# Moving the scaling and the PSUM reads of a quantised feed-forward stage from VectorE to ScalarE

## The reference, cut to what matters

```python
def act_quant(x):
    scale = 127.0 / jnp.clip(jnp.max(jnp.abs(x), axis=-1, keepdims=True), 1e-05)
    return jnp.clip(jnp.round(x * scale), -128, 127) / scale
def bit_linear(x, w):            # wq: ternary weights times one scale
    return jnp.einsum('bsd,hd->bsh', act_quant(x), weight_quant(w))
h = bit_linear(x, w1)                      # 1024 -> 4096
h = silu(depthwise_conv1d(h, conv_w, conv_b))   # 3 taps along the sequence
return bit_linear(h, w2)                   # 4096 -> 1024
# and then: x = layernorm(x + that)
```

## Time and profile before

| | us |
|---|---|
| median of the runs shown (6380.81 and 6395.15) | 6387.98 |
| the profiled execution | 6394.97 |
| its span, core 5, first to last instruction | 6393.4 |
| spans of the eight cores | 6309.8 to 6393.4 |
| from the first memset of the tile loop (4062.6) to the end | 2331 |
| one tile, from one store of y to the next (289.5 each) | 8 of them |

### The profile page before, as it was taken

One profiled execution on the slowest core, in us unless ns is written; L12 is line 12 of the kernel. 1 busy time (PEld: TensorE's weight loads), 2 busy tenths in 40 slices (PEclk: granted clock), 3 DMA queues, 4 the chain that ended last, 5 costly groups with the idle time before them and its releaser, 6 DMA issues.

```text
span 6393.4 us, 40611 instructions; the slowest of 8 cores (6309.8 to 6393.4 us)
## 1 busy us (share of the span) xinstructions
PE 2245.9 (35%) x11808; PEld 1178.4 (18%) x11808; DVE 1953.2 (31%) x3386; ACT 875.4 (14%) x1647; POOL 1499.9 (23%) x1336
## 2 busy tenths in 40 slices
PE   1345432653644543555740000123323232313333
PEld 0111110221211211222320000113222121212222
DVE  0013342332333343221143332233333333333332
ACT  0000032332322223211030000000000000000010
POOL 0000030110110123333241212133333423333333
PEclk8665555776766775777865555556665665656665
DMA  9840034003011010000105332300000000000000
GB/s 154 100 56 0 1 58 113 1 22 84 1 50 49 1 54 14 14 14 14 27 14 209 143 118 89 126 0 14 0 14 7 7 14 0 14 0 14 1 7 7
DMA packets 129593, 258.94 MB, mean 41 GB/s; under 512 B 16705, under 2 KB 79298, under 8 KB 124482
## 3 DMA queue, kind: packets, MB, share of 16 engines
q1 hardware_dynamic: 78786, 202.23, 9.9%
q0 software_dynamic: 50592, 54.11, 6.5%
HBM read 268.22 MB, written 42.21 MB: 49 GB/s over the span
## 4 chain that ended last, share of the span: by engine, by line
PE 33%; DVE 19%; DMA 17%; POOL 16%; issue 8%; ACT 6%; DVEq 1%; SPq 1%; POOLq 0%; ACTq 0%; another core or an unknown queue 0%
PE p4pm L120 8%; PE psm L120 7%; PE p3psv L120 6%; POOL p4tB L136 5%; POOL p4tA L136 4%; DMA xkv<-xT 4%; DVE p4tA L136 3%; DMA wqsw2T<-w2T 3%; POOL XB L136 3%; DVE Y L136 2%; DVE X L136 2%; DMA wqsw1T<-w1T 2%; DMA qbuf<-qTw 2%; PE p4pt L123 1%; DMA p4x<-xspill 1%
## 5 line engine op out<-in xcount | busy, mean ns | idle before, releaser
L136 POOL TENSOR_TENSOR p4tB<-p4h,cw 128x512 f32<-128x512 bf16 x256 | 330.9, 1292 | 553.1 <-DVE p4h L136 310.9
L136 POOL TENSOR_TENSOR Y<-Y,p2asb 128x416 f32<-128x416 f32 x120 | 144.4, 1236 | 1225.0 <-ACT p2bsb L127 1225.0
L120 PE MATMUL p4pm<-p4xq,w1q 128*128 128x260 bf16 x2048 | 260.6, 293 | 430.7 <-DVE p4h L136 415.9
L120 PE MATMUL p4pm<-p4c,w2q 128*128 128x256 bf16 x2048 | 245.8, 287 | 312.0 <-DVE p4c L140 312.0
L120 PE MATMUL p3psv<-XB,w3w 128*128 128x416 bf16 x1280 | 276.8, 386 | 191.4 <-POOL XB L136 190.9
L120 PEld LDWEIGHTS p4pm<-p4xq,w1q 128*128 128x128 bf16 x2048 | 208.6, 104 | 482.8 <-issue 435.0
L120 PEld LDWEIGHTS p4pm<-p4c,w2q 128*128 128x128 bf16 x2048 | 209.8, 103 | 351.6 <-issue 317.6
L136 DVE TENSOR_TENSOR p4tA<-p4tA,p4tB 128x512 f32<-128x512 f32 x256 | 177.1, 692 | 292.4 <-POOL p4tB L136 292.2
L123 PE MATMUL p4pt<-idenb,p4c 128*128 128x128 bf16 x512 | 64.8, 306 | 505.8 <-ACT p4c L132 423.1
L136 POOL TENSOR_TENSOR XB<-X,a3sb 128x416 bf16<-128x416 f32 x160 | 164.8, 1063 | 309.0 <-ACT a3sb L127 309.0
L136 POOL TENSOR_TENSOR p4tA<-p4c,p4tB 128x512 f32<-128x512 bf16 x128 | 148.1, 1157 | 369.7 <-ACT p4tB L127 224.1
(11 more groups left out here) (255 smaller groups left out, 4320.4 us busy)
## 6 DMA issues: line engine op xcount, KB each, us to landing
xkv<-xT POOLq DMA_DIRECT2D x32, 1024.0 KB, 16.9
wqsw1T<-w1T SPq DMA_DIRECT2D x16, 2048.0 KB, 9.3
wqsw2T<-w2T SPq DMA_DIRECT2D x64, 512.0 KB, 3.6
qbuf<-qTw SPq DMA_DIRECT2D x96, 256.0 KB, 3.8
sbuf<-sTe SPq DMA_DIRECT2D x96, 256.0 KB, 4.4
xspill<-X SPq DMA_DIRECT2D x2, 8320.0 KB, 26.9
X<-xin SPq DMA_DIRECT2D x1, 8320.0 KB, 47.1
xrb<-xspill SPq DMA_DIRECT2D x5, 1664.0 KB, 10.6
```

The lines of the kernel that those rows point to most:

```text
L120: e.matmul(o, l, r, start=s, stop=p), inc, 1)
L136: e.tensor_tensor(o, a, b, p), inc, 1)
```

## The change

Everything is in `emit_phase4`.

1. The product with the dequantising scale leaves the read of PSUM and goes into the last step of each quantisation: the tensor-scalar that subtracted MAGIC becomes a scalar-tensor-tensor, `(x - MAGIC) * scale`, both for `xq` (8 per tile) and for `cbuf` (16 per tile).
2. The reads of PSUM become plain copies on ScalarE: 32 per tile for the first product, 8 for the second. For the first two of each half, ScalarE waits for the convolution (`p4cv`) where VectorE did.
3. The casts of x and those of y4n, 8 and 8 per tile, are all done by ScalarE. VectorE and GpSimd no longer wait for them; GpSimd gets a wait for `p4xd` in `p4_front_b`.
4. The no-op and the semaphore `p4yb` go. In the convolution the waits for `p4he` and (new) `p4oe` stand only at `qq` = 0; in the later steps only that for `p4cq` is left. In the quantisation of `cbuf` GpSimd waits for `p4cq` only at `qq` = 0.
5. One memset gets a semaphore, and VectorE waits for it once.

```diff
-        engs = ("scalar", "vector", "gpsimd")
-        for eng in engs:
-            k.wait(eng, "p4xd", vx)
-            k.wait(eng, "p4hm", k.val("p4hm"))
-            k.wait(eng, "ns_qs", k.val("ns_qs"))
+        k.wait("scalar", "p4xd", vx)
+        k.wait("scalar", "p4hm", k.val("p4hm"))
+        k.wait("scalar", "ns_qs", k.val("ns_qs"))
         for ch in range(DCH):
-            k.cp(engs[ch % 3], xq[b][:, ch * TW:(ch + 1) * TW],
+            k.cp("scalar", xq[b][:, ch * TW:(ch + 1) * TW],
                  xc[b][:, ch * TW:(ch + 1) * TW], inc="p4cst")
...
-            k.tsc("vector", xq[b][:, ch * TW:(ch + 1) * TW], sl, MAGIC, None,
-                  ALU.subtract, inc="p4qa0")
+            k.stt("vector", xq[b][:, ch * TW:(ch + 1) * TW], sl, -MAGIC,
+                  rb1[b][:, TW:2 * TW], ALU.add, ALU.mult, inc="p4qa0")
...
-                k.wait("vector", "p4hm", k.val("p4hm"))
+                k.wait("scalar", "p4hm", k.val("p4hm"))
                 if hc16 < 2:
-                    k.wait("vector", "p4cv", k.val("p4cv"))
-                k.tt("vector", hbuf[:, hc16 * TW:(hc16 + 1) * TW], pm[:],
-                     rb1[b][:, TW:2 * TW], ALU.mult, inc="p4he")
+                    k.wait("scalar", "p4cv", k.val("p4cv"))
+                k.cp("scalar", hbuf[:, hc16 * TW:(hc16 + 1) * TW], pm[:], inc="p4he")
...
                 for eng in ("vector", "gpsimd"):
-                    k.wait(eng, "p4he", vhe)
+                    if qq == 0:
+                        k.wait(eng, "p4he", vhe)
+                        k.wait(eng, "p4oe", k.val("p4oe"))
                     k.wait(eng, "p4cq", k.val("p4cq"))
-                    k.wait(eng, "p4yb", k.val("p4yb"))
...
-            k.wait("gpsimd", "p4cq", vcq)
+            if qq == 0:
+                k.wait("gpsimd", "p4cq", vcq)
...
-            k.tsc("vector", c3, tA3, MAGIC, None, ALU.subtract, inc="p4hqw")
+            k.stt("vector", c3, tA3, -MAGIC, r3b, ALU.add, ALU.mult, inc="p4hqw")
...
-            k.wait("vector", "p4om", k.val("p4om"))
-            k.wait("vector", "p4yb", k.val("p4yb"))
-            v1 = k.tt("vector", tB[:, 0:OW], pm[:, 0:OW], tB[:, 3 * OW:4 * OW], ALU.mult,
-                      inc="p4oe")
+            k.wait("scalar", "p4om", k.val("p4om"))
+            k.wait("scalar", "p4y", k.val("p4y"))
+            v1 = k.cp("scalar", tB[:, 0:OW], pm[:, 0:OW], inc="p4oe")
...
-            k.wait("vector", "p4y", k.val("p4y"))
-            k.nopi("vector", "p4yb")
...
-        engs = ("scalar", "vector", "gpsimd")
-        for eng in engs:
-            k.wait(eng, "p4y", vy)
+        k.wait("scalar", "p4y", vy)
         for ch in range(DCH):
-            k.cp(engs[ch % 3], xq[b][:, ch * OW:(ch + 1) * OW],
+            k.cp("scalar", xq[b][:, ch * OW:(ch + 1) * OW],
                  y4n[:, ch * OW:(ch + 1) * OW], inc="p4yc")
```

More of the change, by code:

```diff
@@ L1369, in emit_phase4 @@
     k.memset("vector", cmt[:], 0.0)
-    k.memset("vector", cmtF[:], 0.0)
+    k.memset("vector", cmtF[:], 0.0, inc="p4mz")
+    k.wait("vector", "p4mz", k.val("p4mz"))
     def p4_front_a(t):
@@ L1417, in p4_front_b @@
         vcm = k.val("p4cmd")
+        k.wait("gpsimd", "p4xd", k.val("p4xd"))
         k.wait("vector", "p4red", k.val("p4red"))
@@ L1589, in p4_back @@
             r4b = tB[:, 2 * OW:3 * OW].unsqueeze(1).broadcast_to([128, 2, OW])
+            r3b = tB[:, 3 * OW:4 * OW].unsqueeze(1).broadcast_to([128, 2, OW])
             c3 = cbuf[:].rearrange("p (c w) -> p c w", c=32)[:, q0:q0 + 2, :]
             tA3 = tA[:].rearrange("p (c w) -> p c w", c=2)
-            k.wait("gpsimd", "p4cq", vcq)
+            if qq == 0:
+                k.wait("gpsimd", "p4cq", vcq)
             k.wait("gpsimd", "p4hqw", k.val("p4hqw"))
```

## The result

| | before | after |
|---|---|---|
| median of all runs | 6372.44 us (10 runs, 6356.57 to 6395.15) | 6430.91 us (11 runs, 6416.61 to 6454.37) |
| the profiled execution's span | 6393.4 us | 6415.1 us (core 4) |
| one tile, store to store, mean of 8 cores | 289.23 us (288.8 to 289.7) | 296.14 us (295.7 to 296.5) |

The ratio is 1.0095 with a 95% interval of 1.0077 to 1.0112. On the median before this is +60 us, between +49 and +71. The forecast was +62 and a time of 6450, in a range of 6415 to 6488.

A forecast was written before the change was run, and what follows sets the result against it. The prediction took the kernel to be bound by a serial chain of engines taking turns, none full. Its terms summed to +61.8 us, 6456.8 on the profiled execution, forecast as 6450 us against the runs' median; range 6415 to 6488.

The forecast's parts named there:

- Quantisation of cbuf: Second VectorE link of each step, 427 ns, becomes a 692 ns scalar-tensor-tensor, 128 times, all on the path: +33.9 us.
- Of xq: The same swap at 260 columns, 296 to 428 ns, 64 times: +8.4 us; bounds 0 and +13.6.
- Casts of x and y: Eight casts in a row on ScalarE end later than on three engines: +11.4 us for x, +11.0 for y.
- The side effect on the norm's sums: Norm's matmuls start later after the y casts, so more run at TensorE's slow clock: +1 us.
- Restart: Second half's first product: ScalarE must finish the last Silu before the read that lets TensorE go on: +5.1 us.
- Waits: Convolution steps 1 to 7: one wait fewer behind the blocking one, 0.07 us each, 112 times: -7.8 us.
- Reads: PSUM reads moved to ScalarE are hidden behind TensorE; only the last of each half gain: -1.2 us.
- starving: First product's steady chunks: ScalarE's reads hold up TensorE, +22 us, or +190 with lower clock; chances 0.03 up to +128, 0.03 over.
- Cancelling: Scalar-tensor-tensor as fast as the tensor-scalar in both quantisations: 20 us left, about +4 with waits at bound; chance 0.11.
- A gain of over 2%: Would take -128 us; VectorE's 256 removed PSUM reads, 109 us, all on the path wouldn't suffice; chance 0.01.

The follow-up runs named there:

- The run without the second tensor: Changed kernel with the last step of both quantisations a tensor-scalar again, the dequantising scale left out; ratio 1.0005 (0.9983 to 1.0028).

## Why the stages can't hide each other: the chain cut

The quantisation of cbuf has one scratch tile `tA`, while the first half of `tB` lies idle. With both in turn GpSimd can multiply for the next step while VectorE rounds.

```diff
-            tA3 = tA[:].rearrange("p (c w) -> p c w", c=2)
-            k.wait("gpsimd", "p4hqw", k.val("p4hqw"))
+            tQ = tA[:] if qq % 2 == 0 else tB[:, 0:QW4]
+            tA3 = tQ.rearrange("p (c w) -> p c w", c=2)
+            k.wait("gpsimd", "p4hqw", k.val("p4hqw") - (2 if qq > 0 else 0))
```

Both roundings work on `tQ` too. In the kernel before, the edit also leaves GpSimd's wait for `p4cq` at step 0 alone, as the change does. In the changed kernel and in the kernel before:

> The changed kernel with two scratch tiles in turn in the quantisation of cbuf, so that GpSimd multiplies for the next step while VectorE rounds this one. If the two engines truly overlap, a step takes about 1.3 us (GpSimd 1.16, VectorE 0.43 + 0.69 and gaps) instead of 2.64, -170 us, and the scalar-tensor-tensor costs nearly nothing. If they hold each other up, as the 1.04 us GpSimd operation of the convolution that takes 1.56 beside VectorE suggests, a step takes the sum of the busy times, 2.28: -46 us.

> The kernel before with the same two scratch tiles. Overlapping: 1.25 us a step instead of 2.37, -140 us. Holding each other up: 1.16 + 0.43 + 0.43 = 2.02 a step, -45 us. Beside the run of the changed kernel with two tiles this gives the price of the scalar-tensor-tensor where the chain is cut: about 0.05 us a step if they overlap, 0.26 if they don't.

Measured: 0.9939 (0.9921 to 0.9957) for the changed kernel with two tiles, 0.9841 (0.9817 to 0.9865) for the kernel before with two tiles: 99 us and 101 us gained, by the ratios; by the tile it is 87 and 84 us over eight. The distance between the two versions is still 0.98%. A step takes neither of the values I gave. Timelines of the kernel before, then of the changed kernel, each with two tiles:

```profile
4547.23 1.21 POOL L136 TENSOR_TENSOR p4tB<-p4c,p4tB 128x512 f32<-128x512 bf16 x1 [0.43 <-DVE p4c L140]
4547.53 1.19 DVE L140 TENSOR_SCALAR p4c<-p4tA 128x512 bf16<-128x512 f32 x1
4548.64 0.41 DVE L140 TENSOR_SCALAR p4tB<-p4tB 128x512 f32<-128x512 f32 x1
4548.86 1.21 POOL L136 TENSOR_TENSOR p4tA<-p4c,p4tB 128x512 f32<-128x512 bf16 x1 [0.43 <-DVE p4c L140]
```

```profile
4527.72 1.21 POOL L136 TENSOR_TENSOR p4tB<-p4c,p4tB 128x512 f32<-128x512 bf16 x1 [0.69 <-DVE p4c L144]
4528.02 1.46 DVE L144 SCALAR_TENSOR_TENSOR p4c<-p4tA,p4tB 128x512 bf16<-128x512 f32 x1
4529.40 0.41 DVE L140 TENSOR_SCALAR p4tB<-p4tB 128x512 f32<-128x512 f32 x1
4529.62 1.21 POOL L136 TENSOR_TENSOR p4tA<-p4c,p4tB 128x512 f32<-128x512 bf16 x1 [0.69 <-DVE p4c L144]
```

VectorE's second rounding starts while GpSimd multiplies and ends 0.28 us (tensor-scalar) or 0.55 us (scalar-tensor-tensor) after GpSimd's end: it lasts 1.19 and 1.46 us in place of 0.43 and 0.69. Only the first rounding, which began before GpSimd did, runs beside it. So a step is about GpSimd's 1.21 plus the second rounding: 1.63 and 1.90 us. In full it is GpSimd's 1.21, the 0.28 or 0.55 to the rounding's end, and 0.14 to GpSimd's next start. The difference, 0.27, is the whole price of the scalar-tensor-tensor: cutting the chain of dependencies doesn't cover it, since the second rounding doesn't run beside the multiplication. The Trainium skill, SBUF — State Buffer, section SBUF: two separate sides, says that GpSimd and VectorE share one pair of ports as an exclusive lock: whichever operation starts first holds it to its end, and the other blocks. On VectorE's side it names operations in a two-port mode, and those with two inputs in SBUF against a GpSimd operation that reads SBUF. The two timelines agree with it where GpSimd starts first, with 0.76 and 0.77 us more than the rounding takes alone. Where VectorE starts first they agree only in part: the first rounding ends 0.19 us after GpSimd's start, and GpSimd's operation is only 0.05 longer for it (1.21 against 1.16).

**One rounding instruction.** If each link counts whole, the cheapest gain is to take one out. The two roundings can be one tensor-scalar of two operations, where the scale isn't folded in; this starts from the kernel before without the waits.

```diff
-            vq2 = k.tsc("vector", tA[:], tA[:], MAGIC, None, ALU.add, inc="p4hqw")
-            k.wait("vector", "p4hqw", vq2)
-            k.tsc("vector", c3, tA3, MAGIC, None, ALU.subtract, inc="p4hqw")
+            k.tsc("vector", c3, tA3, MAGIC, MAGIC, ALU.add, ALU.subtract, inc="p4hqw")
```

> The kernel before without the two waits of steps 1 to 7 of the convolution, and with the addition and the subtraction of MAGIC in one tensor-scalar of two operations, in both quantisations. Theory of the serial chain: one VectorE link and its gap fall away, 0.53 us in 128 steps and 0.40 in 64, 94 us, with the waits 103: about 6270, 1.6% under before. If a second operation in one instruction costs time, less.

Measured: 0.9838 (0.9823 to 0.9852), 6270.5 us, -103 by the ratio, as forecast. The tensor-scalar with two operations takes 0.43 us like the one with a single operation, and a step 1.83:

```profile
4524.58 1.16 POOL L136 TENSOR_TENSOR p4tA<-p4c,p4tB 128x512 f32<-128x512 bf16 x1 [0.68 <-DVE p4c L140]
4525.84 0.43 DVE L140 TENSOR_SCALAR p4c<-p4tA 128x512 bf16<-128x512 f32 x1 [1.41 <-POOL p4tA L136]
4526.41 1.16 POOL L136 TENSOR_TENSOR p4tA<-p4c,p4tB 128x512 f32<-128x512 bf16 x1 [0.68 <-DVE p4c L140]
```

**One rounding, and two tiles in both quantisations.** The edit is that of the two scratch tiles with `- (1 if qq > 0 else 0)`, on top of the one rounding, and `tF` and `tA[:, 0:TW]` in turn for `xq`.

> The kernel with one rounding instruction and without the waits, now with two scratch tiles in turn in both quantisations. By the rule read from the two-tile runs (GpSimd's 1.21 us holds up VectorE's next 0.43) a step of cbuf takes 1.6 us instead of 1.83, and one of xq about 1.1 instead of 1.28: 16 x 0.2 + 8 x 0.2 a tile, about -35 us, 6235. If the engines overlapped: 1.2 and 0.8, -110 us.

Measured: 0.9726 (0.9711 to 0.9740), 6201.65 us; by the ratios 71 us under the run before it, twice the 35 I forecast. The stretch of cbuf is 22.3 us, 1.39 a step, and that of xq 6.69 after 9.80. That is better than the 1.6 I took from the two-tile runs:

```profile
4523.59 1.21 POOL L136 TENSOR_TENSOR p4tA<-p4c,p4tB 128x512 f32<-128x512 bf16 x1 [0.43 <-DVE p4c L140]
4524.76 1.16 POOL L136 TENSOR_TENSOR p4tB<-p4c,p4tB 128x512 f32<-128x512 bf16 x1
4524.90 1.30 DVE L140 TENSOR_SCALAR p4c<-p4tA 128x512 bf16<-128x512 f32 x1 [1.12 <-POOL p4tA L136]
4526.12 0.41 DVE L140 TENSOR_SCALAR p4c<-p4tB 128x512 bf16<-128x512 f32 x1
```

GpSimd does two multiplications in a row, the blocked rounding follows, and the other one runs beside the next multiplication. One rounding of two is held up, not each. I had carried the rule over as if every step were like that. In xq a step is 0.83, near the 0.8 I had written for engines that overlap, though there too every second rounding is held up (0.73 us in place of 0.30): the held one ends only 0.14 us after GpSimd's multiplication, so GpSimd's two multiplications of 0.73 fill most of the 1.67 us of two steps.

**The bias left to the Silu.** The last step applies the same reading to the convolution: GpSimd's addition of the bias (1.04 us, line 136, and its signal) is a link that ScalarE can take into the Silu at the price of a second activation.

```diff
-                v6 = k.tt("gpsimd", tA3, tA3, cb3, ALU.add, inc="p4cv")
-                k.act(cbuf[...2 chunks...], tA[:], AF.Silu, inc="p4cq")
+                for c2 in range(2):
+                    k.act(cbuf[...1 chunk...], tA[:, c2 * OW:(c2 + 1) * OW],
+                          AF.Silu, bias=cb4[:, cc:cc + 1], inc="p4cq")
```

> As the run with one rounding and two tiles, and GpSimd's addition of the convolution's bias is left to ScalarE: two Silu of 256 columns, each with its bias, in place of one of 512 and the addition. By the serial chain a step of the convolution loses 1.04 + 0.14 and gains the second Silu, about 0.3: -0.85 us in 128 steps, -110 us, about 6130, 3.8% under before.

Measured: 0.9526 (0.9504 to 0.9548), 6080.21 us, 121 us under the run before it where I expected 110; the tile 250.90 us. One step, Silu to Silu, is 5.53 us, where it was 6.43 in the run before it and 6.50 in the kernel before:

```profile
4701.06 0.91 ACT L132 ACTIVATE p4c<-p4tA,cb 128x256 bf16<-128x256 f32 x2 [4.62 <-DVE p4tA L136]
...
4706.59 0.91 ACT L132 ACTIVATE p4c<-p4tA,cb 128x256 bf16<-128x256 f32 x2 [4.62 <-DVE p4tA L136]
```

A step loses 0.90 us beside the 0.85 of the forecast. The two stretches of the convolution are 7.5 us shorter each, which is 15.1 of the 15.4 us by which the tile falls against the run before it (266.29). This run and the two above it beat the changed kernel and the kernel before.

## Why the prediction was right, point by point

Per eight tiles, from the table of stretches, beside the term of the sum:

- *Quantisation of cbuf:* forecast +33.9, measured +35.1. *Of xq:* +8.4 and +8.2; the duration without a row of its own, 428 ns taken from VectorE's read of PSUM, came out at 429. That this sum fits so well is in part luck. I booked eight steps a tile at 0.132 us; x is loaded right behind GpSimd's eighth multiplication, so only seven count, and each got 0.142 longer (1.686 to 1.828, mean of all cores). The run without the second tensor confirms both (41 us in its stretches).
- *Casts of x and y:* +11.4 and +11.0, measured +11.4 and +10.8. The pitch of 0.31 us read from three copies held for eight (2.58 and 2.55 us). The side effect on the norm's sums, put at +1, was +0.6.
- *Restart:* +5.1, measured +3.7. The step that was mis-sized is the start of the copy: I let it begin at the Silu's end, and it began 0.09 earlier; the signal was 0.12 and not 0.14. The rest is my choice of the tile: in the earlier trace rows TensorE restarted 0.52 after the Silu's start, in the mean of the tiles 0.58.
- *Waits:* -7.8, measured -8.8 in the convolution's stretches; a step is 0.07 shorter, Silu to Silu (6.495 to 6.427, medians), and 0.07 x 112 is the term. The run with only the waits removed shows that the gain comes from them and not from the freed VectorE.
- *Reads:* -1.2, measured -3.2 in the three product stretches. With the same product work in all of them, the sum of the three is 64.83 us a tile before, 64.43 after, 65.47 with the casts given back, 65.01 without the second tensor, 64.11 with only the reads moved, 64.76 with only the waits removed. In the first half alone the seven tiles of one core after lie between 16.06 and 17.83. The windows view shows why, its columns as in the earlier trace rows: first these two tiles (core 4 after), then the second half's product before, just behind the restart of the earlier trace rows and later.

```profile
5266.71:5282.77 16.06, 16.06 (x137) 13.60 (x137) 1.23 (x2) 6.00 (x16) 0.00 (x0) 0.94 0.00 1
4672.90:4690.73 17.83, 17.83 (x138) 14.40 (x138) 1.24 (x2) 6.01 (x16) 0.00 (x1) 0.86 0.01 1
5047.36:5051.10 3.74, 3.74 (x18) 2.60 (x19) 0.63 (x3) 0.11 (x1) 0.00 (x0) 0.50 0.00 0
5052.50:5063.00 10.50, 9.66 (x87) 7.95 (x84) 5.14 (x13) 0.00 (x0) 0.04 (x1) 1.00 0.01 2
```

Behind the restart TensorE begins the product at a granted clock of 0.50, the lower of its two levels, and VectorE's reads start 1.74 us apart (5049.36 and 5051.10); later the clock is 1.00 and they are 0.89 apart. How far into the stretch the clock rises differs from tile to tile. Taking off each stretch its length times one minus its granted clock leaves what it would last at the full clock. The sum of the three is then 58.43 before, 58.27 after, 58.34 with the casts given back, 58.26 without the second tensor, 58.22 with only the reads moved and 58.51 with only the waits removed. So ScalarE's reads are worth about 0.2 us a tile, -1.3 us over eight, and the booked -1.2 holds. The other 1.9 of the 3.2 us are the clock, as is the 1.0 us by which the products are longer with the casts given back. What sets the moment of the rise, no run here tests.

- *Rivals:* starving is refuted by 0.89 us between reads and by the run with only the reads moved. Cancelling is refuted by the 692 ns. A gain of over 2% would have needed the reads to lie on the path, and moving them alone gives 0.9979.

The profiled execution that the sum stood on was 7 us above the median known then and is 22 above the median of ten; so the forecast time of 6450 is 19 above the measured one while the difference, 62 against 60, is right. Each term missed by 2 us or less, and the misses partly cancel; the ratio's interval of 49 to 71 could not have told a fit within 2 us from one within 10.

## What to carry to other kernels

Where the profile shows engines taking turns on one scratch tile, price a move by each instruction's new length as a link and its number of uses; the idle share of the engine that takes it says nothing here (ScalarE was on 6% of the chain and the move still lost time). Folding a multiplication into an existing instruction isn't free if it turns a one-tensor form into a two-tensor form (427 to 692 ns here), and spreading short copies over engines is worth keeping where all wait for the last. The same reading shows what to remove. In all, against the kernel before: one link fewer per step and the waits gone gave 1.6%, two scratch tiles on top of that 2.7%, and the bias taken into the activation on top of both 4.7%. And a difference of 1 us in a stretch of matmuls is first to be held against its granted clock.

## What the runs showed of the hardware that I hadn't expected

- Which of VectorE and GpSimd starts first decides whether they overlap on SBUF tiles of 128x512: a rounding that started during a multiplication lasted 1.19 us in place of 0.43, the two-tensor one 1.46 in place of 0.69; yet a rounding that started 0.22 before the multiplication ran beside it in 0.41 and cost GpSimd 0.05 (1.21 against 1.16).
- A tensor-scalar with two operations takes as long as one with one, 0.43 us for 128x512.
- One satisfied wait behind a blocking one cost 0.07 us on VectorE and 0.06 on GpSimd (medians from the Silu's end, 0.171 to 0.102 and 0.203 to 0.142).
- Of the three product stretches, 5.9 to 7.1 us a tile went to TensorE's lower granted clock in the six kernels listed under *Reads*; at the full clock the six agree within 0.3 us (58.22 to 58.51).
- With two PSUM buffers and chunks of 0.893 us, a read of 0.375 us was hidden and two in a row made the chunk 1.065; by the working above, an estimate, the limit is near 0.49 us.
